# Mixture gating computed by ScalarE straight from PSUM, with the limit applied behind it, and the linear half's bias added by a picking product on TensorE

## The reference, cut to what matters

```
p1 = nf @ mlp1_weight[e].T + mlp1_bias[e]          # 256 -> 512, for each expert e
g = jnp.minimum(p1[..., 0::2], LIMIT)               # LIMIT = 7.0
lin = jnp.clip(p1[..., 1::2], -LIMIT, LIMIT)
act = g * jax.nn.sigmoid(ALPHA * g) * (lin + 1.0)   # ALPHA = 1.702
p2 = act @ mlp2_weight[e].T + mlp2_bias[e]
combined = sum over e of p2 * combine[e]
```

## Time and profile before

| | |
|---|---|
| median of 3 runs | 2372.37 us (2369.58 to 2373.74) |
| the profiled execution | 2370.43 us |
| its span, first to last instruction | 2368.7 us |
| busy in the span: PE, DVE, ACT, POOL | 2102.1, 1471.8, 1031.8, 605.0 us |
| mean granted clock of PE | 0.943 of 2.4 GHz |

### The profile page before, as it was taken

One profiled execution on the slowest core, in us unless ns is written; L12 is line 12 of the kernel. 1 busy time (PEld: TensorE's weight loads), 2 busy tenths in 40 slices (PEclk: granted clock), 3 DMA queues, 4 the chain that ended last, 5 costly groups with the idle time before them and its releaser, 6 DMA issues. The chain is left out here.

```text
span 2368.7 us, 54589 instructions
## 1 busy us (share of the span) xinstructions
PE 2102.1 (89%) x22556; PEld 1733.0 (73%) x22556; DVE 1471.8 (62%) x3140; ACT 1031.8 (44%) x2036; POOL 605.0 (26%) x594
## 2 busy tenths in 40 slices
PE   6999999999999998788887579999868999958885
PEld 4777777777777776667775468999858999956773
DVE  6666666666666664489889645555435454525885
ACT  3666656665666663234333233424224243313442
POOL 1000000000000000166666613343302433424552
PEclk9999999999999999899998779999979999979996
DMA  7001111010101012111200030000021000002000
GB/s 247 15 10 52 43 59 46 17 43 16 46 17 43 12 38 93 56 37 38 65 19 10 18 131 15 12 20 12 11 98 52 29 16 29 12 29 97 10 10 19
DMA packets 59991, 97.17 MB, mean 41 GB/s; under 512 B 7720, under 2 KB 50480, under 8 KB 57392
## 3 DMA queue, kind: packets, MB, share of 16 engines
q1 hardware_dynamic: 53760, 71.98, 9.3%
q10 hardware_dynamic: 5984, 21.69, 2.3%
HBM read 70.45 MB, written 23.20 MB: 40 GB/s over the span
## 5 line engine op out<-in xcount | busy, mean ns | idle before, releaser
L734 DVE CUSTOM_DVE_ANT_0 a_sm<-psum,a_strip 128x1024 f32<-128x1024 f32 x256 | 311.8, 1218 | 33.1 <-PE psum L577 33.1
L662 ACT ACTIVATE a_sm<-a_sm,a_mn 128x1024 f32<-128x1024 f32 x256 | 293.4, 1146 | 29.5 <-DVE a_mn L734 29.4
L667 ACT ACTIVATE a_pT<-psum 128x512 f32<-128x512 f32 x256 | 152.8, 597 | 302.6 <-PE psum L590 302.6
L590 PE MATMUL psum<-ident,a_sm 128*128 128x128 f32 x2048 | 280.0, 280 | 1.1 <-ACT a_pT L667 1.0
L590 PEld LDWEIGHTS psum<-ident,a_sm 128*128 128x128 f32 x2048 | 219.8, 141 | 83.6 <-issue 57.5
L741 DVE COPY a_pT<-psum 128x512 f32<-128x512 f32 x256 | 176.3, 689 | 131.7 <-PE psum L590 131.7
L605 PE MATMUL psum<-a_pT,a_V 128*64 128x256 f32 x2048 | 249.0, 385 | 1.3 <-DVE a_o L752 1.3
L1150 POOL TENSOR_TENSOR b_x_in<-b_x_in,b_bo_a 128x512 f32<-128x512 f32 x8 | 10.2, 1277 | 911.0 <-POOLq L528 911.0
L605 PEld LDWEIGHTS psum<-a_pT,a_V 128*64 128x64 f32 x2048 | 135.7, 136 | 77.7 <-issue 22.1
L1038 PE MATMUL psum<-b_w,b_act_hi 128*128 128x256 f32 x256 | 64.7, 337 | 59.3 <-POOL b_act_lo L1138 59.3
L577 PE MATMUL psum<-a_KH,a_QH 64*128 64x512 f32 x512 | 114.6, 443 | 2.5 <-DVE a_mn L734 2.5
(11 more groups left out here) (379 smaller groups left out, 4584.8 us busy)
## 6 DMA issues: line engine op xcount, KB each, us to landing
a_strip<-table SPq DMA_DIRECT2D x16, 960.0 KB, 6.7
oT<-a_o SPq DMA_DIRECT2D x64, 128.0 KB, 1.9
b_oT_in<-oT SPq DMA_DIRECT2D x8, 1024.0 KB, 5.5
a_raw<-in_a_wqkv SPq DMA_DIRECT2D x7, 384.0 KB, 3.4
s_x<-in_x_rev SPq DMA_DIRECT2D x4, 512.0 KB, 7.5
vb<-s_zero SPq DMA_DIRECT2D x8, 256.0 KB, 2.9
b_x_in<-in_x SPq DMA_DIRECT2D x8, 256.0 KB, 5.6
b_vb_in<-vb SPq DMA_DIRECT2D x8, 256.0 KB, 5.6
```

The lines of the kernel that those rows point to most:

```text
L590: last = pe.transpose(psum[:, 4 + j, k * P:(k + 1) * P], sm[:, st % RING, kt * P:(kt + 1) * P], ident[:, :])
L662: a.activation(sm[:, st % RING, :], sm[:, st % RING, :], ACT.Exp, scale=-1.0, bias=mn[:, at:at + 1], accum_out=rsum[:, at:at + 1]).then_in ...
L667: a.activation(probs(st, 0), psum[:, 4, :].rearrange("p (k q) -> p k q", k=4), ACT.Copy).then_inc(sig("pT_act"), 1)
L734: v.tensor_tensor_reduce(out=sm[:, st % RING, :], in0=scores_banks(hl).rearrange("p c n -> p (c n)"), in1=strip[:, pair % 2, hl, qt * P:qt ...
```

## The change

The gate half is no longer touched by DVE and POOL. ACT reads it from PSUM and applies `Gelu_apprx_sigmoid` (x times sigmoid(1.702 x)) with the bias column, in two instructions of 256 columns. The limit is put on the result: the minimum with 7/(1 + exp(-1.702 * 7)), in the instruction that forms `act`, whose second operand becomes the already clipped `lin`. The linear half gets its bias on PE: the transposed biases `b1r` (16 rows of biases, 16 of zeros and one row of ones) are multiplied by `pick`, which holds a one in the row of the expert's bias and a one in the last row, so that bias + 1 is added to the sum in PSUM. DVE then clips that half from both sides in one instruction of 512 columns. `b1r` is made in step 0 and 1 by a transpose on PE and a copy on DVE, `pick` by a memset and a copy on DVE at the end of step 0. x times sigmoid(1.702 x) grows with x from zero on, so its minimum with its value at 7 stands for the limit on x.

```diff
-        b1b, b1 = sb("b1b", [P, E0, 2, KC], BF16), sb("b1", [P, E0, 2, KC])
+        b1b, b1 = sb("b1b", [P, E0, 2, KC], BF16), sb("b1", [P, E0, KC])
+        NB, ONE = E0 * KC, 32
+        b1l, b1r, pick = sb("b1l", [P, NB]), sb("b1r", [ONE + 1, P], BF16), sb("pick", [ONE + 1, NB, CP], BF16)
...
-        gate, lin, sg, gs = (sb(n, [P, ER, KC, CP]) for n in ("gate", "lin", "sg", "gs"))
+        lin, gs = (sb(n, [P, ER, KC, CP]) for n in ("lin", "gs"))
...
-                    units += [("m1", 2 * (p * E0 + n) + i) for i in range(2)]
+                    units += [("ug", p * E0 + n), ("ul", p * E0 + n)]
...
+            if s == 0:
+                units += [("br", 0)]
...
                 def up(s, e):
                     pe.wait_ge(have("w1"), 16)
-                    for part in range(2):
-                        bank = banks.take(pe, "m1", 2 * (s * E0 + e) + part)
+                    pe.wait_ge(sig("ones"), 4)
+                    pe.wait_ge(sig("br_out"), 1)
+                    for part, stage in enumerate(("ug", "ul")):
+                        bank = banks.take(pe, stage, s * E0 + e)
                         for m in range(KC):
                             at = e * 2 * I0 + part * I0 + m * P
+                            half = bank[:, m * CP:(m + 1) * CP]
                             for k in range(KC):
-                                last = pe.matmul(bank[:, m * CP:(m + 1) * CP], w1[:, k, at:at + P], nT[:, s % 2, k, :],
-                                                 start=k == 0, stop=k == KC - 1)
-                        last.then_inc(sig("m1_ps"), 1)
+                                last = pe.matmul(half, w1[:, k, at:at + P], nT[:, s % 2, k, :],
+                                                 start=k == 0, stop=part == 0 and k == KC - 1)
+                            if part:
+                                last = pe.matmul(half, b1r[:, :], pick[:, e * KC + m, :], start=False, stop=True)
+                        last.then_inc(sig(f"{stage}_ps"), 1)
...
+                    if s == 0:
+                        pe.wait_ge(sig("wide"), 1)
+                        pe.transpose(banks.take(pe, "br", 0)[0:NB, 0:P], b1l[:, :], ident[:, :]).then_inc(sig("br_ps"), 1)
...
-                def sigmoid(s, e):
+                def gated(s, e):
                     n = s * E0 + e
-                    a.wait_ge(sig("m_gate"), n + 1)
+                    a.wait_ge(sig("ug_ps"), n + 1)
                     if n >= ER:
-                        a.wait_ge(sig("m_gs"), n - ER + 1)
-                    a.activation(sg[:, n % ER, :, :], gate[:, n % ER, :, :], ACT.Sigmoid, scale=ALPHA).then_inc(sig("m_sig"), 1)
+                        a.wait_ge(sig("m_act"), n - ER + 1)
+                    for m in range(KC):
+                        last = a.activation(gs[:, n % ER, m, :], banks("ug", n)[:, m * CP:(m + 1) * CP],
+                                            ACT.Gelu_apprx_sigmoid, bias=b1[:, e, m:m + 1])
+                    last.then_inc(sig("ug_out"), 1)
...
-                        sigmoid(q, 0)
-                        sigmoid(q, 1)
+                        a.wait_ge(sig("wide"), 1)
+                        gated(q, 0)
+                        gated(q, 1)
                         high(q, 0)
-                        sigmoid(q, 2)
+                        gated(q, 2)
                         high(q, 1)
...
-                def gated(s, e):
-                    n = s * E0 + e
-                    g.wait_ge(sig("m_sig"), n + 1)
-                    if n >= ER:
-                        g.wait_ge(sig("m_act"), n - ER + 1)
-                    g.tensor_tensor(gs[:, n % ER, :, :], gate[:, n % ER, :, :], sg[:, n % ER, :, :], ALU.mult).then_inc(sig("m_gs"), 1)
...
                     if back:
-                        gated(q, 1)
                         low(q, 0)
-                        gated(q, 2)
                     if front:
                         norm_rstd(g, sig, "bn", s, bn, mhalf)
                     if back:
                         low(q, 1)
-                        gated(q, 3)
...
                 def clipped(s, e):
                     n = s * E0 + e
-                    v.wait_ge(sig("m1_ps"), 2 * n + 1)
+                    v.wait_ge(sig("ul_ps"), n + 1)
                     if n >= ER:
-                        v.wait_ge(sig("m_gs"), n - ER + 1)
                         v.wait_ge(sig("m_act"), n - ER + 1)
-                    for m in range(KC):
-                        last = v.tensor_scalar(gate[:, n % ER, m, :], banks("m1", 2 * n)[:, m * CP:(m + 1) * CP],
-                                               b1[:, e, 0, m:m + 1], LIMIT, ALU.add, ALU.min)
-                    last.then_inc(sig("m_gate"), 1)
-                    v.wait_ge(sig("m1_ps"), 2 * n + 2)
-                    for m in range(KC):
-                        last = v.tensor_scalar(lin[:, n % ER, m, :], banks("m1", 2 * n + 1)[:, m * CP:(m + 1) * CP],
-                                               b1[:, e, 1, m:m + 1], LIMIT + 1.0, ALU.add, ALU.min)
-                    last.then_inc(sig("m1_out"), 2)
+                    v.tensor_scalar(lin[:, n % ER, :, :], halves(banks("ul", n)), LIMIT + 1.0, 1.0 - LIMIT,
+                                    ALU.min, ALU.max).then_inc(sig("ul_out"), 1)
 
                 def activated(s, e):
                     n = s * E0 + e
-                    v.wait_ge(sig("m_gs"), n + 1)
-                    v.wait_ge(sig("m1_out"), 2 * (n + 1))
+                    v.wait_ge(sig("ug_out"), n + 1)
+                    v.wait_ge(sig("ul_out"), n + 1)
                     if n >= 2:
                         v.wait_ge(sig("m_lo"), n - 1)
-                    v.scalar_tensor_tensor(act[:, e % 2, :, :], lin[:, n % ER, :, :], 1.0 - LIMIT, gs[:, n % ER, :, :],
-                                           ALU.max, ALU.mult).then_inc(sig("m_act"), 1)
+                    v.scalar_tensor_tensor(act[:, e % 2, :, :], gs[:, n % ER, :, :], LIMIT / (1.0 + math.exp(-ALPHA * LIMIT)),
+                                           lin[:, n % ER, :, :], ALU.min, ALU.mult).then_inc(sig("m_act"), 1)
...
+                    if s == 1:
+                        v.wait_ge(sig("ones"), 1)
+                        v.wait_ge(sig("br_ps"), 1)
+                        v.tensor_copy(b1r[0:NB, :], banks("br", 0)[0:NB, 0:P]).then_inc(sig("br_out"), 1)
...
                         v.wait_ge(have("w2b"), 16 * 3)
                         v.tensor_copy(b2[:, :], b2b[:, :])
-                        v.tensor_copy(b1[:, :, 0, :], b1b[:, :, 0, :])
-                        v.tensor_scalar(b1[:, :, 1, :], b1b[:, :, 1, :], 1.0, None, ALU.add)
+                        v.tensor_copy(b1[:, :, :], b1b[:, :, 0, :])
+                        v.tensor_copy(b1l[:, :].rearrange("p (e k) -> p e k", e=E0), b1b[:, :, 1, :])
                         v.tensor_copy(w2[:, :, :, :], w2b[:, :, :, :]).then_inc(sig("wide"), 1)
+                        v.memset(b1r[0:ONE, :], 0.0).then_inc(sig("ones"), 1)
+                        v.memset(b1r[ONE:ONE + 1, :], 1.0).then_inc(sig("ones"), 1)
+                        v.memset(pick[ONE:ONE + 1, :, :], 1.0).then_inc(sig("ones"), 1)
+                        v.tensor_copy(pick[0:ONE, :, :], ident[0:ONE, 0:NB].rearrange("p (n o) -> p n o", o=1).broadcast_to([ONE, NB, CP])).then_inc(sig("ones"), 1)
```

18 lines of the change are left out of this document (6 added, 12 removed).

## The result

The changed kernel takes 2356.7 us (median of 4 runs, 2355.0 to 2357.3), the kernel before beside it 2371.0 (2367.5 to 2373.7): a ratio of 0.9939, with a 95% interval of 0.9922 to 0.9957. That is 14 us faster. The forecast was 2342 us, 29 us faster. The profiled execution took 2357.0 us, with a span of 2355.2. Busy in it: PE 2130.6 us (28.5 more than before), DVE 1394.3 (77.5 less), ACT 1053.1 (21 more), POOL 512.8 (92 less).

A forecast was written before the change was run, and what follows sets the result against it. It took DVE as what is full, with PE waiting and then running slowly behind its waits. Full steps -23, step 8 -7, step 9 -6.5 and start +7 gave -29.5 us: 2341, or 2342 for the median, between 2330 and 2354.

The forecast's parts named there:

- What bounds the kernel: Full steps: DVE is full at 41.2 of 46.1 us; PE's 40.9 is soft, since part ran at 1.2 GHz.
- the meetings: DVE instructions slowed where POOL works at the same time, in full steps; fewer meetings save up to 2 us a step.
- The full steps, -23 for six: Six full steps of the phase, 46.3 us each, fall by 3.8 to 42.5 us, 23 us in all.
- its columns are the same, so I take 0.116: PE's bias products: 33 rows priced like other 256-column bf16 matmuls, 0.116 us each, 1.9 us a step at 2.4 GHz.
- The first landmark: Full step, from up 0 to the end of `ay`: 0.7 us later, by the bias of three ups.
- the biases cost more than their columns: Slower rival: PE's 33-row products cost extra, deciding from 0.29 us beyond 0.116; about 2385 at 0.4 beyond; chance 0.07.
- Step 8, -7, and step 9, -6.5: Last two steps: DVE sheds work and POOL's gating leaves the end chain; 7.0 and 6.5 us saved, bounds 3.5 and 9.
- The start, +7: Step 1: DVE's memset, cast and small instructions delay the `ay` sum by 7 us, between 5.2 and 9.3.
- The memset: DVE's memset of 4096 elements at the start of the phase: 4.3 us taken, with 2.27 as the low end.
- The table load, +0.1 a step: ACT's third table load of 1.28 us uses up a 1.24 us wait for DVE, coming out 0.1 us late a step.
- The rival that a switch holds ACT for 2.6 us: A second 1.28 us per switch delays `high` 4 and down 4 in seven steps; 9 us lost, 2351; chance 0.05.
- The rival that PE is the bound already: DVE's gain becomes PE waits: 1 us a step, 4 for each of the last two, 8 lost at start; 2365; chance 0.17.

The follow-up runs named there:

- with 128 rows: The changed kernel with the bias product widened from 33 to 128 rows, the added rows of the bias table being zeros; median 2335.9 us.
- With the start off the path as well: The changed kernel with 128-row bias products and the start's table writing, transpose and copy moved off DVE's path; median 2324.5 us.

## Why the prediction was off, step by step

- **What bounds the kernel.** Right that PE's busy time was soft, and that the `ay` sum stood late for reasons of DVE. Of the reasons, POOL's leg weighed more than the clips, and the prediction had it the other way round: "up to 2 us a step" for the meetings, where the leg as a whole was worth 3.9 when put back, and 5.4 us of DVE's work 1.0.
- **The full steps, -23 for six.** They gave -24.8: -2.3 in step 2 and -4.5 in each of the others. The sum was right for the wrong amounts. That is luck. The bias products took 2.1 us a step more than counted, POOL's leg was worth 2 more, and the low clock that had fallen on `bq` went, which was worth up to 2.
- **The failed step: "its columns are the same, so I take 0.116".** A product of 33 rows costs 0.116 + 0.21 us. The first landmark shows it: from up 0 to the end of `ay` the forecast had 0.7 us more, and 1.9 came; with 128 rows it is 0.6. With 128 rows the median is 2335.9, inside the forecast's own range of 2330 to 2354 and 6 us under its 2342. The rival "the biases cost more than their columns" had the mechanism, and a price of 0.29 us beyond the columns from which it would decide; it came at 0.21 and took 18.0 of the 36.0 us that the phase would have won. (That price is worked out from the gain of 37 without the start's 7; from the net gain of 29.5 it is 0.23. And 0.4 us beyond the columns would make 51 us, 2393 and not 2385.) Its nearest row, the first matmul of an expert, was no neighbour of it. The trace of before has a nearer one, the load for the 8-row fp32 products of `mb`, which stand in each step behind the 128-row ones of `ay`: it stood idle for 2.4 us in 8 times. In step 4 the first of them starts 0.31 us behind the last of `ay`, whose own starts are 0.22 apart. It is a hint only, since `mb` also waits for semaphores there.
- **Step 8, -7, and step 9, -6.5.** They gave -3.3 and -0.9, the largest miss by stretches. In both the products of 33 rows stand in PE's queue among the `up` and `down` that the chain waits for: with 128 rows step 9 is 3.2 us shorter, and step 8 only 0.7, at a lower clock (0.71 in place of 0.75). With the start off the path as well, which gives both steps a higher clock, the two are at -5.9 and -4.3, 10.2 of the 13.5 us. Without any bias product they are at -6.8 and -4.6, so 2 to 3 us of the 13.5 were over-sized.
- **The start, +7.** DVE's part was right to 0.1 us (6.9), in part by luck: the memset took 0.8 us less than the 4.3 counted, and an idle time of 0.80 us ahead of it, which nothing in the sum had, made up for it. What hung on it was not: PE's longer idle time lengthened its stretch at the low clock, another 4.1 us. In all the start's work cost 11.1 in step 1, and 13.8 of the phase.
- **The memset.** It took 3.47 us for 4096 elements of bf16 in one partition, and as long in 64 and in 128, between my bounds of 2.27 and 4.3. The Trainium skill (VectorE: DVE Perf Modes, Zero memsets can be issued as uint32) has one cycle an element whatever the type, an estimate of 4.3 us; the row is a fifth under that.
- **The table load, +0.1 a step.** 0.2, measured.
- **The rival that a switch holds ACT for 2.6 us** fell: down 4 waited 1.51 us with two loads and 1.71 with three.
- **The rival that PE is the bound already** has the measured time in its range, 2354 to 2366, but not by its terms: it had 1 us a full step, and 4.1 came on average. PE did become nearly full (40.35 of 42.04 us at full clock), by products that cost nearly three times what was counted, and not because of what it did before: with 128 rows it is busy 37.2 of 39.9 us, and the time falls to 2335.9.

What was to show it: L1213 at 0.69 us, DVE busy 30 us a step, full steps of 42 to 43, PE's clock over 0.93, waits for `low` under 40 us and the `ay` sum right behind `ay` (0.1 us) all came, and all went together with half the gain. Down 4 waited 1.20 us, not 1.5 to 2, since PE came to it later. One sign of being wrong came, L1037 against L1034, and that was the cause of the larger part; the other part is the low clock of step 1.

What stays open: why the low clock of the kernel before falls where it does, and so how much of the full steps' gain would be left in an execution of before with steps of 44.4 us; why steps 8 and 9 have clocks from 0.71 to 0.82 and from 0.68 to 0.89 over these kernels; and what it is in a switch between products of fewer rows and of 128 that takes the 0.21 us, since only 33, 64 and 128 rows were tried, each among products of 128.
